# The turned q and k ahead of the v projections in each slot, and the clip of the norms as a maximum with a constant tensor

## The reference, cut to what matters

```
qkv = shift_token(x) @ wqkv                       # 8 heads of 64
q = q / clip(norm(q), 1e-12) * q_scale            # the same for k
q, k = rotary_xpos(q, k)
o = local_attention(q, k, v)                      # windows of 64 tokens, each looks at itself and the one before
x = x + o @ wo
x = x + w2(a * gelu(g)),  a, g = layernorm(shift_token(x)) @ w1
```

## Time and profile before

| | |
|---|---|
| median of three runs | 4263.49 us |
| lowest, highest | 4258.25, 4268.59 us |
| the profiled execution, its own time | 4274.6 us |
| its span (first to last instruction) | 4272.7 us |
| mean granted TensorE clock | 0.902 of full speed |
| busy: PE, DVE, ACT, POOL | 77%, 59%, 60%, 40% of the span |
| PE matmul records | 17248 |

### The profile page before, as it was taken

How to read it: one execution, slowest core, us unless ns; L and a number is a source line. 1 busy time by engine, 2 the same in 40 slices (tenths; PEclk the granted TensorE clock), 3 DMA queues, 4 the chain that set the end, 5 groups by cost and what they waited for, 6 DMA issues and landing times. The chain is left out here.

```text
span 4272.7 us, 57448 instructions
## 1 busy us (share of the span) xinstructions
PE 3276.9 (77%) x17248; PEld 1946.2 (46%) x17248; DVE 2528.6 (59%) x4239; ACT 2573.8 (60%) x5843; POOL 1726.7 (40%) x1428
## 2 busy tenths in 40 slices
PE   4677878777787877777777787777878777777777
PEld 2354445444444444444544444444444444445443
DVE  5564665657556565666646656575565656666443
ACT  4456567665666655666655666656666556665554
POOL 2353343524425353343533435244253533435332
PEclk8788998988999889898988989889998898989899
DMA  2000000000000000000000000000000000000000
GB/s 81 3 1 1 6 1 6 1 1 6 1 6 1 1 6 1 6 1 1 6 1 6 1 6 1 1 6 1 6 1 1 6 1 6 1 1 3 1 3 3
DMA packets 18387, 20.57 MB, mean 5 GB/s; under 512 B 768, under 2 KB 17152, under 8 KB 17792
## 3 DMA queue, kind: packets, MB, share of 16 engines
q1 hardware_dynamic: 18048, 16.44, 1.2%
HBM read 12.24 MB, written 4.19 MB: 4 GB/s over the span
## 5 line engine op out<-in xcount | busy, mean ns | idle before, releaser
L1448 POOL TENSOR_TENSOR hc<-hst,Cs 128x512 f32<-128x512 f32 x512 | 655.4, 1280 | 1136.0 <-DVE hst L1218 1029.1
L1218 DVE TENSOR_TENSOR_SCAN hst<-dA,bank 128x512 f32<-128x512 f32 x512 | 624.8, 1220 | 266.9 <-issue 144.5
L560 PE MATMUL bank<-W,xs 128*128 128x512 f32 x960 | 511.2, 681 | 21.4 <-DVE tmp L1359 19.7
L912 ACT COPY Cs<-bank 128x512 f32<-128x512 f32 x512 | 298.9, 584 | 291.2 <-PE bank L543 261.8
L543 PE MATMUL bank<-parts,sel 96*128 96x512 bf16 x1024 | 353.2, 417 | 136.3 <-ACT Cs L912 63.9
L1044 ACT ACTIVATE Pm<-bank,mx 128x128 f32<-128x128 f32 x1024 | 363.1, 370 | 145.8 <-DVE mx L1379 145.8
L1522 POOL TENSOR_TENSOR Pm<-Pm,rinv 128x512 f32<-128x512 f32 x256 | 271.4, 1060 | 426.7 <-DVE rinv L1372 403.7
L1210 DVE TENSOR_TENSOR bank<-u,bank 128x512 f32<-128x512 f32 x512 | 350.6, 685 | 151.6 <-PE bank L543 149.7
L1507 POOL TENSOR_TENSOR oT<-tmp 128x512 f32<-128x512 f32 x256 | 325.2, 1270 | 257.8 <-DVE tmp L1359 194.7
L906 ACT ACTIVATE dA<-delta,neg_a 128x512 f32<-128x512 f32 x512 | 371.7, 726 | 48.3 <-DVE hst L1218 47.4
L528 PE MATMUL bank<-C,hc 128*128 128x128 f32 x2048 | 344.3, 296 | 35.9 <-POOL hc L1448 35.8
(11 more groups left out here) (223 smaller groups left out, 6163.7 us busy)
## 6 DMA issues: line engine op xcount, KB each, us to landing
W<-wpack SPq DMA_DIRECT2D x1, 4498.0 KB, 13.6
x_tok<-x SPq DMA_DIRECT2D x16, 256.0 KB, 2.9
out<-xa SPq DMA_DIRECT2D x16, 256.0 KB, 2.2
rot<-tables SPq DMA_DIRECT2D x2, 512.0 KB, 16.2
wc_f<-taps SPq DMA_DIRECT2D x1, 1024.0 KB, 19.4
C<-cpack SPq DMA_DIRECT2D x1, 721.0 KB, 14.8
Pm<-mask SPq DMA_DIRECT2D x1, 320.0 KB, 15.1
tmp<-rowpack SPq DMA_DIRECT2D x1, 256.0 KB, 17.2
```

The lines of the kernel that those rows point to most:

```text
L560: mm(b[:, :], weights, rhs, start=True, stop=True).then_inc(full(ring, job), 1)
L912: nc.scalar.copy(Cs[:, k % 2, :], b[:, :]).then_inc(sem("a_Cs"), 1)
L1218: v.tensor_tensor_scan(o, a, b, 0.0, ALU.mult, ALU.add).then_inc(sem("a_h"), 1)
L1448: g_.tensor_tensor(hc[:, k % 2, :], hst[:, k % 2, :], Cs[:, k % 2, :], ALU.mult)\
```

## The change

```diff
--- before.py
+++ after.py
@@ -85,9 +85,10 @@
         _n = _s - UNIT
         if _s < NT:
             B_JOBS += [(f"q{_l}{_s}", "t_sin", 8 * _l + 2 * _s + 1), (f"k{_l}{_s}", "t_sin", 8 * _l + 2 * _s + 2)]
-            B_JOBS += [(f"v{_l}{_w}", "t_v", 7 * _l + _w) for _w in (2 * _s + 1, 2 * _s + 2) if _w < NW]
         if 2 <= _s < 2 + NT:
             B_JOBS += [(f"qt{_l}{_s - 2}", "t_q", 8 * _l + 2 * _s - 2), (f"kt{_l}{_s - 2}", "t_k", 4 * _l + _s - 1)]
+        if _s < NT:
+            B_JOBS += [(f"v{_l}{_w}", "t_v", 7 * _l + _w) for _w in (2 * _s + 1, 2 * _s + 2) if _w < NW]
         if 0 <= _n < NU:
             B_JOBS += [(f"S{_l}_{_n}", "t_exp", NU * _l + _n + 1)]
         if LAG_T <= _n < NU + LAG_T:
@@ -121,6 +122,7 @@
 OUT = 3
 HOME = {f"{name}{k}": k % 2 if name == "B" else 2 for name in "BC" for k in range(2 * NS)}
 HOME |= {f"v{l}{at}": OUT for l in range(NL) for at in range(2, NW, 2)}
+HOME |= {f"kt{l}{s}": OUT for l in range(NL) for s in range(NT)}
 HOME["G"] = OUT
 
 
@@ -291,6 +293,7 @@
         tmp1 = sb("tmp1", [2, T])
         tmp2 = sb("tmp2", [2, T])
         ssq = sb("ssq", [NT, 2, HA])
+        least = sb("least", [2, HA])
         rqk = sb("rqk", [NT, 2, HA])
         mx = sb("mx", [2, 4])
         rsum = sb("rsum", [2, 4])
@@ -700,6 +703,8 @@
                     def project(s):
                         for kind in ("q", "k"):
                             norm_sum("B", f"{kind}{l}{s}", i, xsh[:, s * P:(s + 1) * P], w(f"w{kind}{l}"))
+
+                    def project_v(s):
                         for at in (2 * s + 1, 2 * s + 2):
                             if at < NW:
                                 norm_sum("B", f"v{l}{at}", i, xsh[:, (at - 1) * WIN:(at + 1) * WIN], w(f"wv{l}"))
@@ -744,10 +749,11 @@
                     def weigh(n):
                         half, g = UNITS[n]
                         pe.wait_ge(*step("t_PT", i, NU * l + n + 1))
-                        if g == 0:
-                            pe.wait_ge(*step("t_v", i, 7 * l + (3 if half == 0 else 7)))
+                        if n > 0 and g == 0:
+                            pe.wait_ge(*step("t_v", i, 7 * l + 7))
                         if n == 0:
                             pe.wait_ge(*step("t_v", i, 7 * l + 6))
+                            pe.wait_ge(*step("t_k", i, 4 * l + 4))
                         elif n % 2 == 0:
                             pe.wait_ge(*step("t_oT", i, 4 * l + n // 2))
                         for wi in range(4):
@@ -767,6 +773,8 @@
                             project(s)
                         if 2 <= s < 2 + NT:
                             channel_major(s - 2)
+                        if s < NT:
+                            project_v(s)
                         if 0 <= n < NU:
                             scores(n)
                         if LAG_T <= n < NU + LAG_T:
@@ -1008,12 +1016,6 @@
                             f(rqk[:, s - 1], ssq[:, s - 1], ACT.Ln).then_inc(sem("t_rln"), 1)
                             act.wait_ge(*step("t_rln", i, 4 * l + s))
                             f(rqk[:, s - 1], rqk[:, s - 1], ACT.Exp, scale=-0.5).then_inc(sem("t_r"), 1)
-                        if s < NT:
-                            for at in (2 * s + 1, 2 * s + 2):
-                                if at < NW:
-                                    act.wait_ge(*filled("B", f"v{l}{at}", i))
-                                    b = bank("B", f"v{l}{at}")
-                                    nc.scalar.copy(vt[:, at - 1, :], b[:, :]).then_inc(sem("t_v"), 1)
                         if 2 <= s < 2 + NT:
                             at = s - 2
                             act.wait_ge(*filled("B", f"qt{l}{at}", i))
@@ -1026,6 +1028,12 @@
                             b = bank("B", f"kt{l}{at}")
                             nc.scalar.copy(kT[:, :, at * P:(at + 1) * P], b[:, :].rearrange("p (g t) -> p g t", g=4))\
                                 .then_inc(sem("t_k"), 1)
+                        if s < NT:
+                            for at in (2 * s + 1, 2 * s + 2):
+                                if at < NW:
+                                    act.wait_ge(*filled("B", f"v{l}{at}", i))
+                                    b = bank("B", f"v{l}{at}")
+                                    nc.scalar.copy(vt[:, at - 1, :], b[:, :]).then_inc(sem("t_v"), 1)
                         if LAG_T <= n < NU + LAG_T:
                             k = n - LAG_T
                             act.wait_ge(*filled("B", f"PT{l}_{k}", i))
@@ -1099,6 +1107,7 @@
             done(v.memset(inv256[:, :], 1.0 / DI))
             done(v.memset(col_eps[:, :], EPS))
             done(v.memset(col_one[:, :], 1.0))
+            done(v.memset(least[:, :, :], 1e-24))
             done(v.memset(hpad[:, :], 0.0))
             done(v.memset(xs0[:, :], 0.0))
             done(v.memset(qbd[:, :, :, :], 0.0))
@@ -1363,7 +1372,7 @@
                                 v.tensor_reduce(ssq[:, s, kind, :], sq[:, kind, :].rearrange("p (h d) -> p h d", h=HA),
                                                 AX.X, ALU.add).then_inc(sem("t_ss"), 1)
                             dve.wait_ge(*step("t_ss", i, 8 * l + 2 * s + 2))
-                            v.tensor_scalar(ssq[:, s], ssq[:, s], 1e-24, None, ALU.max).then_inc(sem("t_clip"), 1)
+                            v.tensor_tensor(ssq[:, s], ssq[:, s], least[:, :, :], ALU.max).then_inc(sem("t_clip"), 1)
                         if 1 <= n < NU + 1:
                             k = n - 1
                             dve.wait_ge(*step("t_exp", i, NU * l + k + 1))
@@ -1528,7 +1537,7 @@
             run(pool, prologue, scan, head, stage_b, finish)
 
 
-SETUP = 7 + 4 + 3 + 2 + TAPS + 1 + 2 + len(TABLES) * NL
+SETUP = 1 + 7 + 4 + 3 + 2 + TAPS + 1 + 2 + len(TABLES) * NL
```

## The result

The changed kernel takes **4321.03 us** (median of 4 runs, 4314.92 to 4326.15) where the kernel before takes 4263.06 beside it: ratio 1.0134, 95% interval 1.0118 to 1.0150. That is slower by 58 us. The forecast was 4245 and the range ended at 4284. The profiled execution's span is 4324.3 us, 51.6 over the one before.

The account below looks back on a forecast made before the run. No engine is near full; a chain through all engines was taken to bound the kernel. Layer 0's -0.65 and layer 1's -0.56 gave -1.21 us per image, times 15 images 18.2 us: median 4245 us, range 4216 to 4284.

Parts of the forecast that it names:

- Turned tiles ahead of v, layer 0: -0.65: Slots 2 and 3 of layer 0: PE's second stop goes, q3, k3 and norms come sooner, -0.65 us per image.
- Layer 1: -0.56: Slots 2 and 3 of layer 1: q3 later but full clock back sooner, -0.56 us per image, bounds +0.76 to -2.43.
- The clip's form costs nothing: Clip as tensor_tensor maximum on DVE: still stands behind POOL as the old form does, 0 us.
- clip set free: Rival, 5%: the new clip is not held by POOL, 35 us more gained, 4210 us.
- v, kT and rotation cost nothing: Later v copies, last copy of kT and changed bank rotation: covered by slots of slack, no cost.
- half clock in layer 0: Rival, 20%: PE falls to half clock around v5, v6 and q3 of layer 0, +1.15 us per image, 4281 us.
- Given back: Rival, 30%: the gain in slots 2 and 3 is real but lost later in the loop body, 4263 us.

Follow-up runs that it names:

- e10: The changed kernel plus two thrown-away PE projections ahead of the turned k in slots 2 and 3 of layer 0 alone: 4286.72 us, ratio 1.0038.
- e17: The changed kernel plus one thrown-away PE projection in each of slots 2 and 3 of layer 0 alone: 4287.92 us, ratio 1.0048.
- e1: The kernel before with only the clip changed to a tensor_tensor maximum, old order and banks kept: 4272.61 us, ratio 1.0010.
- e6: The kernel before with the new order and banks in layer 1 alone, old clip: 4259.43 us, ratio 0.9975.
- e13: The kernel before with new order and two thrown-away projections in slots 2 and 3, both in layer 1 alone, old clip: 4260.10 us, ratio 0.9968.
- e3: The kernel before plus a 912 ns DVE memset (1024 columns) per image ahead of layer 0's first q: 4303.37 us, ratio 1.0081.
- e8: The kernel before plus a 485 ns DVE memset (512 columns) per image ahead of layer 0's first q: 4290.71 us, ratio 1.0047.
- e12: The changed kernel plus one thrown-away PE projection in each of slots 2 and 3 of both layers: 4221.21 us, ratio 0.9872.

## Why the prediction was wrong, point by point

The step that failed is in both terms of the sum and in the weight of one rival: the working took PE's clock as it was before (layer 0) or as coming back sooner (layer 1), and stopped at slot 3. It set against the rival that PE stood 1.73 and 1.20 us there and kept its clock. In its place the runs show 12.6 us more at half clock in each body, and +5.1 us where -1.21 was forecast; with layer 0's stop filled, 33 us or more of the 58 come back (e10, e17).

- **Turned tiles ahead of v, layer 0: -0.65.** Right for the chain at full clock. In image 7, q3 starts 11.19 us behind the first clip (2123.05 - 2111.86) where it did at 11.70, 0.51 sooner, and the clip of slot 3 ends 0.50 sooner. Of the missing 0.14 most is the first projection, whose first record lasts 0.53 us up to the next behind a stop and not 0.43 (v5 and v6 take 2122.18 - 2120.36 = 1.82 and not 1.72). Wrong in that I took the clock as given: eight of the ten bodies of images 3 to 12 have half clock there, and the stretch is 0.78 longer on average.
- **Layer 1: -0.56.** Wrong. In image 7 the clip of slot 0 is at 2205.78, and the norms begin at:

```profile
2223.31 0.21 ACT L1016 ACTIVATE rqk<-ssq 128x16 f32<-128x16 f32 x1
```

  that is 17.53 us behind it, where it was 2200.72 - 2183.13 = 17.59 before: 0.06 gained. v5 and v6 ran at half rate ahead of q3, as I had worked out, and the half clock ended sooner too, 15.6 us behind the clip of slot 0 for 18.4. But q3 began at 2220.13, that is 1.14 later behind that clip and not 0.76 (0.31 of it arose ahead of v5), and q3 and k3 gave back 1.15 and not 1.32, so nothing was left. Over ten bodies the slots of layer 1 are 0.30 longer. And the clip of slot 2, which was free before (2195.72, 0.17 us), now stands behind POOL, in the timelines of DVE and of POOL:

```profile
2218.70 0.89 DVE L1375 TENSOR_TENSOR ssq<-ssq,least 128x16 f32<-128x16 f32 x1
```
```profile
2218.29 1.27 POOL L1516 TENSOR_TENSOR oT<-tmp 128x512 f32<-128x512 f32 x1 [0.58 <-DVE tmp L1368]
```

  because POOL's sums now start earlier. I had noted that they do, and not asked what that collides with.
- **The clip's form costs nothing.** Right, shown by e1 and by the pair of 897 ns. The Trainium skill's rule on two SBUF inputs (SBUF — State Buffer, "SBUF: two separate sides") is borne out: in e1 the tensor_tensor takes 755 ns and not 174, and in the rows above it ends with POOL's sum. The rival "clip set free" fell. The section of the Trainium skill that the prediction set against this rule (VectorE: DVE Perf Modes, "Why tensor_tensor can't do 2×_2P or 4×") says itself that a tensor_tensor reads its second tensor through the second port, so it did not speak for a free clip. And half of the pair's 2.21 us is 1.10, not 1.06, which changes nothing.
- **v, kT and rotation cost nothing.** Nothing in the runs speaks against it; it wasn't tried by itself.
- **The rival "half clock in layer 0" at 4281, 20%.** It named the right place and sign, and its price in layer 0 was near: +0.77 against +0.96 (18.47 - 17.51) in bodies that have it. What failed is the next step, that this and a share for layer 1 are the whole price. The half clock behind it grew too: +1.73 us from there to layer 1 and +2.27 between layer 1 and the next image, neither of which I counted. The working read one image whose neighbours were alike, and took that alikeness for a property of the kernel.
- **"Given back".** It had the 259.4 us as evidence, and e6 and e13 show it at work: gains in layer 1 leave most bodies at 259.4. But the same alikeness can break, which e3, e8 and the changed kernel itself show.

## What to carry to other kernels

When an edit takes away a wait of PE, look at how PE's idle time is divided afterwards: two short stops that merge into one longer one can cost more, by the half clock behind it, than the wait was worth. This is no rule of length: 1.73 and 1.19 us were followed by half clock in e3, and 3.12 us were not in e12. Sum the half clock over whole loop bodies, and not in the changed slots alone. Before believing a gain or a loss of about 1% in a loop, shift the loop body by a fraction of a microsecond and measure again; and where a longer stop of PE can't be avoided, try a matmul in it whose result is thrown away.

## What the runs showed that I had not expected

- The same change in PE's idle time acts far away: with 12.6 us more at half clock per body, 4.0 of the 5.1 us lost lie outside slots 0 to 3, in stretches whose instructions and order are the same; only the banks of slots 4 and 5 and a wait of the first product with v differ.
- A memset of 485 ns per image, 7.8 us in all, made the kernel before 19 us slower; one of 912 ns left the changed kernel within its spread (4323.86 against 4321.03).
- One thrown-away projection in each of four slots took 100 us off, two took less (4252, with the old clip), and most body lengths lie near a few values: about 256, 259.4, 261 to 263 and 264 to 266 us.
